# Group norm of the next image inside the attention, and earlier maxima, in a conv, attention and experts kernel

## The chip, the cores and the metric

The kernel runs on one core of a Trainium2 chip. The metric is the time of one execution on the device, in microseconds. The core has TensorE (PE: matmuls, its weight loads listed as PEld), VectorE (DVE), ScalarE (ACT), GpSimd (POOL) and SyncE (SP), which issues DMAs. The engines run their own instruction streams and meet through semaphores. PSUM, where matmuls put their results, has eight banks of 128 x 512 float32.

## The reference, cut to what matters

For each of 8 images x (192 channels, 32 x 32 = 1024 tokens):

```python
x = x + spiking_attention(group_norm(x))   # 32 groups of 6 channels
t = tokens(x)                              # 1024 x 192
t = t + softmax_attention(layer_norm(t))   # 6 heads of 32, causal
t = t + experts(layer_norm(t))             # 4 experts, 192 -> 768 -> 192, the best 2 by a gate

spike(x) = round(clip(x, 0, 4)) / 4
xs = spike(group_norm(x)); q, k, v = spike(conv_bn(xs)); kv = k^T v (by head, 8 heads)
a = spike(q @ kv * scale); out = conv_bn(a)
gate = softmax(x @ gate_w + gate_b), masked to its two largest, normed to a sum of 1
y = sum_e gate[e] * (gelu(x @ w1[e] + b1[e]) @ w2[e] + b2[e])
```

## The kernel before

An image has two stages. In the **attention** (`attend`) 36 steps j go over (block b of 512 queries, pair of heads, chunk kc of 128 keys). In step j PE makes the scores of item j (L474, L478; banks 4 and 5 or 6 and 7, two steps in turn) and, two items behind, the weighted sums of item j-2 (`weigh`, L676; banks 0 and 1, in turn by run, a run being one block and pair). ScalarE makes the exponential of an item (L875), in five buffers. VectorE norms a run's output in three parts (L1283; L1288 and L1292; L1301, which signals `o_done`), one part a step, from three steps behind the run's last item. The first sums of run r wait for the output of run r-2.

In the **experts** (`experts`) 48 chunks i go over (block, expert, 128 of 768 hidden columns), with three chunks of lag behind them. PE's order in chunk i: the hidden product of i (`hidden`, L439, five matmuls), asides due by i-0.5, the expert output of i-3 (`expert_out`, L729, twelve matmuls into banks 2 and 3; with an expert's last chunk four biases, L734), asides due by i. Where i-3 begins an expert, asides due by i come before its output. ScalarE: GELU of i (L895), a scaled float16 copy (L903), then asides due by i. VectorE: asides due by i-0.5, then after an expert's sixth output the accumulation (`add_expert`, four instructions, L1335), then the low half h_l (L1351), then asides due by i. ScalarE thus serves an aside due at a half step at the chunk's end.

Asides are Python generators. `yield T` means that what follows is due at step T; `Aside.until(step)` emits all that is due by then. So the due times in `FRONT_AT` and `TAIL_AT` put each engine's order down in writing, and each engine waits on semaphores besides. `tail` is the output projection, second layer norm, transposes and gate of a block: block 0's runs in the attention (bank 2 and 3, from 18.5), block 1's in the experts (banks 4 and 5, from 4). `front` of the **next** image runs in the experts of this one:

- group norm: statistics of x by channel (L1052 to L1056), two small products with a group matrix (L494, L498, bank 7) that sum over groups, mean and variance (L1059 to L1072), the power -1/2 on GpSimd (L954), a refining step (L1029 to L1077), Relu with scale and bias on ScalarE (L794), rounding on VectorE (L1084, L1086) into xs;
- query (L510), key and value (L523) products of the spikes, their Relus (L801, L809) and roundings; kvm (L534), its split, the attention products (L547), their rounding (L1117, L1120), the projection (L559), the residual t1 (L1129), the first layer norm: statistics (L1010 to L1024), power on GpSimd (L976), normed blocks u (L1039, L1042), transposes (L446) with copies ah (ScalarE, L815) and al (VectorE, L1152); six query-key products (L439) whose high and low halves are written by ScalarE (L821) and VectorE (L1161); value products (L439) and their copy (L830);
- the heads and keys are spread by 24 + 24 DMAs from SyncE and GpSimd;
- the 36 maxima: products of queries and keys (L617, with a mask L621; banks 4 and 5 or 6 and 7 in turn) whose row maxima VectorE takes (L1169). `maximum_step` places them. Of block 0 they are transposed into rows (L454, L782).

The first image's front runs in the setup by the same table, with the pieces of the weights in between. The GpSimd order in an image is: power of norm 1, keys, power of the tail's two blocks, group power of the next image. SyncE's is: spread, then channels and tokens of the next image.

Of the kernel before, what the change touches and what calls it, by code (L numbers as in the profile page):

```python
# [1 line left out]

# [59 lines left out]
           for half in range(b + 1) for pair in range(PAIRS)]  # L62
# [29 lines left out]

PV_BANK = (0, 1, 0, 1, 0, 1)
# [3 lines left out]
def maximum_step(i):  # L97

    return FRONT_AT["maxima"] + int(2 * i / PER_CHUNK) / 2

# [34 lines left out]
def build(nc, x_ch, x_tok, consts, w_conv, bn, w_in, w_out, b1, b2, gate_b, out):  # L135
    with ExitStack() as ctx:
# [218 lines left out]
        y_used = sem("y_used", NB * EXPERTS)  # L355
# [18 lines left out]
        def _(sp):  # L374
            def load(img):
                sp.wait_ge(xs_ready, at(xs_ready, img, 0))
                sp.dma_start(xc[:, :, :], x_ch[img]).then_inc(x_ch_in, 16)
                sp.wait_ge(t1_ready, at(t1_ready, img, 0))
                sp.dma_start(xt[:, :, :], x_tok[img]).then_inc(x_tok_in, 16)
# [50 lines left out]
        def _(pe):  # L430
# [55 lines left out]

            def front(img, later):


                yield FRONT_AT["sums"]  # L490
                pe.wait_ge(gn_rhs, at(gn_rhs, img, 1))
                if later:
                    pe.wait_ge(e_done, at(e_done, img, 0))
                pe.matmul(ps[0:CC, 7, 0:2], group, gn_s[:, :], start=True, stop=True)\  # L494
                  .then_inc(gn_ps, 1)
                yield FRONT_AT["sums2"]
                pe.wait_ge(gn_rhs, at(gn_rhs, img, 2))
                pe.matmul(ps[0:CC, 7, 2:4], group, gn_v[:, :], start=True, stop=True)\  # L498
                  .then_inc(gn_ps, 1)


                for b in range(NB):
                    yield FRONT_AT["q"] + 2 * b
                    if b == 0:
                        pe.wait_ge(xs_ready, at(xs_ready, img, 2))
                    elif later:
                        pe.wait_ge(gate_used, at(gate_used, img, 0))
                    for m in range(2):
                        for n, (w, c) in enumerate(((wc_h, 0), (wc_l, 0), (wc_h, 1), (wc_l, 1))):
                            mm = pe.matmul(ps[0:CC, 6 - 2 * b + m, :], w[0:CC, c, m * CC:(m + 1) * CC],  # L510
                                           xs[0:CC, c, b * QB:(b + 1) * QB], start=(n == 0), stop=(n == 3))
                        mm.then_inc(q_ps, 1)
                for t in range(NT):
                    if t % 2 == 0:
                        yield FRONT_AT["kv"] + t // 2

                    if t < 4:
# [3 lines left out]
                    for n, (w, c) in enumerate(((wc_h, 0), (wc_l, 0), (wc_h, 1), (wc_l, 1))):  # L521
                        rows = CC + 1 if c == 0 else CC
                        mm = pe.matmul(ps[:, 4 + (t + 2) % 4, 0:2 * C], xs[0:rows, c, t * P:(t + 1) * P],  # L523
# [3 lines left out]
                yield FRONT_AT["kvm"] + 0.5  # L527
# [4 lines left out]
                for m in range(2):  # L532
                    for t in range(NT):
                        mm = pe.matmul(ps[0:CC, 4, m * CC:(m + 1) * CC], kvi[:, t, m * CC:(m + 1) * CC],  # L534
# [4 lines left out]
                for b in range(NB):  # L539
                    yield FRONT_AT["attn"] + b  # L540
# [3 lines left out]
                    pe.wait_ge(q_int, at(q_int, img, b + 1))  # L544
                    for m in range(2):
# [5 lines left out]
                for t in range(NT):  # L551
                    if t % TB == 0:
                        yield FRONT_AT["p"] + t // TB
# [12 lines left out]
                for b in range(NB):  # L566
                    yield FRONT_AT["turn"] + b + 0.5
# [4 lines left out]
                for i in range(QK_PARTS * NB):  # L572
                    b, j = divmod(i, QK_PARTS)
                    yield FRONT_AT["qk"] + i // 2 + (0.5 if i % 2 else 0)
# [8 lines left out]
                for t in range(NT):  # L583
                    if t % 4 == 0:
                        yield FRONT_AT["v"] + t // 4
# [8 lines left out]
                for i, (b, t, half, pair) in enumerate(M_ITEMS):  # L594
                    yield maximum_step(i)
# [36 lines left out]
            def tail(img, b, later):  # L632
# [859 lines left out]
```

## Time and profile before

| what | us |
|---|---|
| median of three runs | 1693.17 (1693.16 to 1693.79) |
| the profiled execution | 1693.13 |
| its span | 1691.2 |
| busy in the span: PE, DVE, ACT | 1594.4, 1186.7, 904.3 |
| one image of the steady middle | 201.3 |

Busy time is the union of an engine's instructions. PE's matmuls are pipelined and their ends modelled, so a group's time on PE is read from start to start. An image's times are shown for the one whose experts begin at 771.6 us; its attention begins at 929.4 us and ends at 973.

### The profile page before, as it was taken

Reading aid. Unit: us, or ns where it says so; the run is one execution under the profiler, and the core shown is the slowest. Engines: PE = TensorE matmul, PEld = TensorE weight load, DVE = VectorE, ACT = ScalarE, POOL = GpSimd, SP = SyncE. Lnnn points to the kernel's source line nnn. Section 1 sums busy time; section 2 is a strip of 40 time slices with the busy share of each in tenths; the row PEclk is TensorE's granted clock in tenths of the full one; section 3 lists DMA queues with packets and bytes.
Section 4 is the critical chain, followed back from the end, with each engine's and each line's share of the span. In section 5 each row is a group of like instructions: output and inputs, shape, how many; then the busy total and the mean of one; then the engine's idle time right before and its main releaser. Section 6 shows DMA issues by size and latency. Waiting matters only on the chain.

```text
span 1691.2 us, 32852 instructions
## 1 busy us (share of the span) xinstructions
PE 1594.4 (94%) x13274; PEld 1032.3 (61%) x13274; DVE 1186.7 (70%) x2537; ACT 904.3 (53%) x1329; POOL 173.4 (10%) x247
## 2 busy tenths in 40 slices
PE   3989999999999999999998999999999999999998
PEld 1534666556765576556775566655666557655666
DVE  6677776767676775868758678676767677586643
ACT  3216654466544655356553665446654566535654
POOL 2300111001300003001020010200120000300100
PEclk9999999999999999999999999999999999999999
DMA  4202001100201002010020100210010100200000
GB/s 159 70 13 64 2 16 52 48 2 2 54 14 48 1 1 66 1 48 1 1 67 1 49 2 3 65 33 17 2 46 21 48 2 1 67 1 11 1 11 10
DMA packets 25130, 47.29 MB, mean 28 GB/s; under 512 B 7410, under 2 KB 16946, under 8 KB 23700
## 3 DMA queue, kind: packets, MB, share of 16 engines
q1 hardware_dynamic: 15728, 27.85, 6.0%
q0 software_dynamic: 6144, 9.45, 2.4%
q10 hardware_dynamic: 3108, 7.91, 1.3%
q8 instruction: 104, 1.70, 0.4%
q14 instruction: 46, 0.38, 0.1%
HBM read 19.82 MB, written 6.29 MB: 15 GB/s over the span
## 4 chain that ended last, share of the span: by engine, by line
PE 67%; DVE 23%; ACT 4%; issue 3%; POOL 1%; DMA 1%; SPq 0%; DVEq 0%; ACTq 0%; POOLq 0%
PE ps L439 20%; PE ps L729 16%; PE ps L676 10%; DVE mx L1169 7%; PE ps L474 6%; DVE acc L1335 3%; PE ps L617 3%; DVE room L1351 3%; PE ps L523 2%; DVE norm_stats L1010 2%; PE ps L510 1%; PE ps L446 1%; ACT room L895 1%; PE ps L478 1%; DVE gn_st L1052 1%
## 5 line engine op out<-in xcount | busy, mean ns | idle before, releaser
L895 ACT ACTIVATE room<-ps,b_sb 128x512 f32<-128x512 f32 x384 | 263.3, 686 | 459.4 <-PE ps L439 459.3
L729 PE MATMUL ps<-wout_h,room 128*128 128x192 f16 x3072 | 459.5, 246 | 5.4 <-DVE acc L1335 5.4
L1351 DVE SCALAR_TENSOR_TENSOR room<-room 128x512 f16<-128x512 f32 x384 | 262.6, 687 | 179.3 <-ACT room L903 174.3
L729 PE MATMUL ps<-wout_l,room 128*128 128x192 f16 x1536 | 378.0, 246 | 0.0
L729 PEld LDWEIGHTS ps<-wout_h,room 128*128 128x128 f16 x3072 | 286.5, 98 | 45.8 <-DVE acc L1335 11.8
L875 ACT ACTIVATE room<-ps 128x1024 f32<-128x1024 f32 (+3 forms) x288 | 225.0, 811 | 157.5 <-PE ps L478 120.1
L1169 DVE TENSOR_REDUCE mx<-ps 128x2 f32<-128x1024 f32 (+3 forms) x288 | 264.2, 950 | 33.7 <-PE ps L621 18.1
L903 ACT ACTIVATE room<-room 128x512 f16<-128x512 f32 x384 | 241.9, 630 | 34.0 <-ACT room L895 0.4
L676 PE MATMUL ps<-room,v 128*64 128x512 f32 (+3 forms) x1152 | 232.6, 488 | 0.9 <-DVE o L1301 0.9
L617 PE MATMUL ps<-qk 96*128 96x512 f16 (+3 forms) x576 | 149.0, 328 | 33.2 <-DVE mx L1169 29.0
L729 PEld LDWEIGHTS ps<-wout_l,room 128*128 128x128 f16 x1536 | 150.4, 98 | 27.4 <-issue 0.3
L474 PE MATMUL ps<-qk 98*64 98x512 f16 (+3 forms) x1152 | 156.1, 331 | 10.8 <-DVE mx L1169 8.0
L439 PE MATMUL ps<-uh,win_h 128*128 128x512 f16 x384 | 146.0, 380 | 2.9 <-DVE o L1301 2.9
L439 PE MATMUL ps<-uh,win_l 128*128 128x512 f16 x384 | 145.6, 379 | 0.0
L439 PE MATMUL ps<-ul,win_t 128*128 128x512 f16 x384 | 145.5, 379 | 0.0
L439 PE MATMUL ps<-uh,win_t 128*128 128x512 f16 x384 | 145.5, 379 | 0.0
L439 PE MATMUL ps<-ul,win_h 128*128 128x512 f16 x384 | 145.5, 379 | 0.0
L1335 DVE SCALAR_TENSOR_TENSOR acc<-ps,gate,acc 128x192 f32<-128x192 f32 x256 | 88.9, 409 | 72.4 <-PE ps L734 71.7
L474 PEld LDWEIGHTS ps<-qk 98*64 98x64 f16 x1152 | 61.9, 110 | 93.2 <-issue 47.1
L982 POOL TENSOR_TENSOR norm_pow<-norm_var,minus_half 128x4 f32<-128x4 f32 x16 | 18.6, 1166 | 911.7 <-DVE norm_var L1024 911.7
L617 PEld LDWEIGHTS ps<-qk 96*128 96x128 f16 x576 | 52.2, 98 | 92.4 <-DVE mx L1169 51.7
L676 PEld LDWEIGHTS ps<-room,v 128*64 128x64 f32 x1152 | 66.4, 137 | 29.9 <-issue 3.0
(203 smaller groups left out, 2314.2 us busy)
## 6 DMA issues: line engine op xcount, KB each, us to landing
xc<-x_ch SPq DMA_DIRECT2D x8, 768.0 KB, 5.9
qk<-qk_all SPq DMA_DIRECT2D x96, 64.0 KB, 2.3
qk<-qk_all POOLq DMA_DIRECT2D x96, 64.0 KB, 2.5
out<-acc ACTq DMA_DIRECT2D x16, 384.0 KB, 2.5
xt<-x_tok SPq DMA_DIRECT2D x7, 768.0 KB, 7.1
qk<-qk_all POOLq DMA_DIRECT2D x96, 32.0 KB, 2.0
qk<-qk_all SPq DMA_DIRECT2D x96, 32.0 KB, 2.4
room<-w_in SPq DMA_DIRECT2D x2, 1024.0 KB, 8.7
```

Source lines behind the costliest of these rows:

```text
L439: mm = pe.matmul(dst, lhs, rhs, start=(n == 0), stop=(n == 4))
L474: mm = pe.matmul(ps[keys, bank, q0:QB], k4[:, h, kc * P + keys.start:kc * P + keys.stop], q4[:, h, b * QB + q0:(b + 1) * QB], start=True, ...
L523: mm = pe.matmul(ps[:, 4 + (t + 2) % 4, 0:2 * C], xs[0:rows, c, t * P:(t + 1) * P], w[0:rows, c, C:3 * C], start=(n == 0), stop=(n == 3))
L617: mm = pe.matmul(ps[:, bank, 0:width], q4[0:3 * D, h, t * P:(t + 1) * P], k4[0:3 * D, h, half * QB:half * QB + width], start=True, stop=no ...
L676: mm = pe.matmul(ps[a * 2 * D:(a + 1) * 2 * D, bank, q0:QB], v32[:, kc * PAIRS + pair, a * D:(a + 2) * D], p32[j % N_P32][:, a, q0:QB], st ...
L729: mm = pe.matmul(dst, hid[:, s, tok], w[:, n, :], start=(k == 0 and m == 0 and t % 2 == 0), stop=False, skip_group_check=True)
L875: act.activation(p32[j % N_P32][:, :, q0:QB], ps[:, bank:bank + 2, q0:QB], ACT.Exp, scale=scale).then_inc(e_done, 1)
L895: act.activation(h32[:, i % N_H, :], ps[:, H_BANK[i], :], ACT.Gelu, scale=1 / (U_SCALE * W_SCALE), bias=b1_sb[:, n:n + 1])\
L903: act.activation(h_h[:, i % N_H, :], h32[:, i % N_H, :], ACT.Copy, scale=A_SCALE)\
L1169: V.tensor_reduce(mx[:, half, t, 2 * pair:2 * pair + 2], ps[:, bank:bank + 2, 0:width], AX.X, ALU.max)\
L1335: ins = V.scalar_tensor_tensor(out=acc[:, n, :], in0=ps[:, 2 + t // 2, (t % 2) * C:(t % 2 + 1) * C], scalar=gate[:, n, e:e + 1], in1=acc[: ...
L1351: V.scalar_tensor_tensor(out=h_l[:, s, :], in0=h32[:, s, :], scalar=A_SCALE, in1=h_h[:, s, :], op0=ALU.mult, op1=ALU.subtract)\
```

## The change

- The front's first part, from the statistics to the spikes xs, is taken out as a generator `early`. For images after the first it runs beside `tail` in the attention of the image before (`EARLY_AT`), with the group sums in bank 2 for bank 7. The projection of the tail's block 0, which uses bank 2 too, waits for the group variance.
- What is left of the front gets its own table: queries 4.5 steps sooner, keys and values 3.5, kvm 3, attention to query-key products 1.5, values 2.5, maxima 5. The maxima are set at 2.1 a chunk (2.75 before). Query, key and value products use banks 6 and 7 alone, each waiting for the Relu two products back; kvm goes to bank 6.
- An expert's output signals after its first two token tiles (`y_half`) and at its end; the accumulation runs in two halves, each behind its signal, and PE's next expert waits for them one by one, bank by bank.
- GpSimd's group power stands before the tail's. SyncE loads the channels of the image after the next once the spikes of the next are made, behind its tokens.
- The first image keeps its table under the name `FIRST_AT`, with 2.1 in place of 2.75, whose order there is the same.

```diff
+FIRST_AT = {... as FRONT_AT was, with "relu": 7.5 and "q1": 12.5 ...}
+EARLY_AT = {"stats": 1, "sums": 6, "sums2": 8, "variance": 8, "clip": 10.5, "relu": 11.5, "xs": 13}
+FRONT_AT = {"q": 6, "q1": 8, "q_int": 7, "kv": 9, "kv_int": 9.5, "kvm": 13.5, "kvm_split": 14.5,
+            "attn": 17, "attn_int": 17, "p": 18, "residual": 18, "norm": 20.5, "turn": 22.5,
+            "high": 23.5, "low": 23.5, "qk": 24.5, "qk_lo": 24.5, "v": 27.5, "maxima": 29.5}
-FRONT_AT = {"stats": 3, "sums": 4.5, "sums2": 5.5, "variance": 5.5, "clip": 6, "xs": 8.5,
-            "q": 10.5, "q_int": 11.5, "kv": 12.5, "kv_int": 13, "kvm": 16.5, "kvm_split": 17.5,
-            "attn": 18.5, "attn_int": 18.5, "p": 19.5, "residual": 19.5, "norm": 22, "turn": 24,
-            "high": 25, "low": 25, "qk": 26, "qk_lo": 26, "v": 30, "maxima": 34.5}
-PER_CHUNK = 2.75
+PER_CHUNK = 2.1
+KVM_BANK = 6
+def group_bank(img):
+    return 2 if img else 7
+def query_bank(later, b, m):
+    return 6 + m if later else 6 - 2 * b + m
+def key_value_bank(later, t):
+    return 6 + t % 2 if later else 4 + (t + 2) % 4
...
             load_later(0)
+            load_channels(1)
             for img in range(B - 1):
                 spread(img)
                 if img == 0:
                     load_later(1)
-                load(img + 1)
+                load_tokens(img + 1)
+                if img + 2 < B:
+                    load_channels(img + 2)
...
+            def early(img, when):                      # PE
+                yield when["sums"]
+                pe.wait_ge(gn_rhs, at(gn_rhs, img, 1))
+                if img > 1:
+                    pe.wait_ge(y_used, at(y_used, img - 1, 0))
+                pe.matmul(ps[0:CC, group_bank(img), 0:2], group, gn_s[:, :], start=True, stop=True)\
+                  .then_inc(gn_ps, 1)
+                yield when["sums2"]
...
                     if b == 0:
                         pe.wait_ge(xs_ready, at(xs_ready, img, 2))
+                        if later:
+                            pe.wait_ge(e_done, at(e_done, img, 0))
                     elif later:
-                        pe.wait_ge(gate_used, at(gate_used, img, 0))
+                        pe.wait_ge(q_relu, at(q_relu, img, 2))
...
+                    if later:
+                        pe.wait_ge(*((q_relu, at(q_relu, img, t + 3)) if t < 2 else
+                                     (kv_relu, at(kv_relu, img, t - 1))))
...
                     pe.wait_ge(q_int, at(q_int, img, b + 1))
+                    if b == 0 and later:
+                        pe.wait_ge(gate_used, at(gate_used, img, 0))
...
                 if b:                                  # tail, PE
                     pe.wait_ge(e_done, at(e_done, img, NE))
+                elif img + 1 < B:
+                    pe.wait_ge(var_ready, at(var_ready, img + 1, 1))
...
+                following = Aside(early(img + 1, EARLY_AT) if img + 1 < B else iter(()))
                 for j in range(NE + PV_LAG):
...
                         weigh(j - PV_LAG)
+                    following.until(j)
                     aside.until(j)
...
-                            pe.wait_ge(y_used, at(y_used, img, i // HC))
+                            pe.wait_ge(y_used, at(y_used, img, 2 * (i // HC) - 1))
                     pe.wait_ge(h_lo, at(h_lo, img, i + 1))
                     s = i % N_H
                     for t in range(TB):
+                        if k == 0 and i and t == TB // 2:
+                            pe.wait_ge(y_used, at(y_used, img, 2 * (i // HC)))
...
+                            if t == TB // 2 - 1:
+                                mm.then_inc(y_half, 1)
...
+            def early(img, when):                      # ACT
+                yield when["relu"]
+                act.wait_ge(gn_ready, at(gn_ready, img, 1))
+                if img:
+                    act.wait_ge(a_int, at(a_int, img, 0))
+                for c in range(2):
+                    yield when["relu"] + c
+                    act.activation(tx[:, c, :], xc[:, c, :], ACT.Relu, scale=g_rstd[:, c:c + 1],
+                                   bias=gn_b[:, c:c + 1]).then_inc(x_relu, 1)
...
+                if img + 1 < B:                        # GpSimd
+                    group_power(img + 1)
                 power_of_tail(0)
...
             def add_expert(y):                         # DVE
                 b, e = divmod(y, EXPERTS)
-                dve.wait_ge(f2_done, at(f2_done, img, (y + 1) * HC))
-                for t in range(TB):
+                for half in range(2):
+                    if half == 0:
+                        dve.wait_ge(y_half, at(y_half, img, y + 1))
+                    else:
+                        dve.wait_ge(f2_done, at(f2_done, img, (y + 1) * HC))
+                    if y:
+                        dve.wait_ge(y_used, at(y_used, img, 2 * y - 1 + half))
+                    for t in range(half * TB // 2, (half + 1) * TB // 2):
...
```

VectorE's `early` holds the old lines from the statistics to the two roundings of xs; in its attention loop `following.until(j)` stands behind the norming of a run's output and ahead of the tail's `aside.until(j)`.

## Rows read from the trace of the kernel before

**Rows 1.** Busy us (x instructions) of each engine, clock, DMA: an image, its maxima.

```profile
771.00:972.30 201.30, 194.07 (x1646) 127.00 (x1644) 144.82 (x314) 111.39 (x165) 20.00 (x29) 1.00 0.09 25
...
875.00:929.40 54.40, 49.26 (x416) 33.08 (x414) 44.89 (x65) 21.66 (x32) 0.00 (x0) 1.00 0.00 1
```

**Rows 2.** Who waited for whom, 771.5 to 875: us, times, longest; TensorE's.

```profile
PEld ps L446 <- DVE u L1042: 1.0, 1, 1.0
...
PEld ps L498 <- DVE gn_v L1069: 0.9, 1, 0.9
PEld ps L729 <- DVE acc L1335: 0.9, 1, 0.9
...
PEld ps L439 <- DVE al L1152: 0.5, 1, 0.5
...
PEld ps L439 <- DVE ul L1213: 0.4, 1, 0.4
```

**Rows 3.** The chain that ended last: start, us, what; first and last of the maxima.

```profile
875.58 1.08 PE ps L439 x5
...
877.12 0.99 PE ps L729 x12
...
929.50 0.23 PE ps L474 x2
```

**Rows 4.** Who waited for whom in the maxima, 875 to 929.4.

```profile
PEld ps L617 <- DVE mx L1169: 5.6, 9, 1.8
```

**Rows 5.** Groups by shape in one image: count, busy us, mean ns, idle before.

```profile
L1351 DVE SCALAR_TENSOR_TENSOR room<-room 128x512 f16<-128x512 f32 x48 | 32.8, 686 | 19.1 <-ACT room L903 18.4 <-PE ps L729 0.5
L1169 DVE TENSOR_REDUCE mx<-ps 128x2 f32<-128x1024 f32 x18 | 21.4, 1217 | 1.6 <-PE ps L617 1.4
L1335 DVE SCALAR_TENSOR_TENSOR acc<-ps,gate,acc 128x192 f32<-128x192 f32 x32 | 11.1, 409 | 9.1 <-PE ps L734 9.0
...
L895 ACT ACTIVATE room<-ps,b_sb 128x512 f32<-128x512 f32 x48 | 32.9, 686 | 60.1 <-PE ps L439 60.0
L903 ACT ACTIVATE room<-room 128x512 f16<-128x512 f32 x48 | 30.2, 630 | 4.2
...
L821 ACT ACTIVATE qk_all<-ps 128x512 f16<-128x512 f32 x6 | 3.5, 589 | 2.6 <-PE ps L439 2.6
...
L794 ACT ACTIVATE tmp<-xc,gn_b,g_rstd 96x1024 f32<-96x1024 f32 x2 | 2.5, 1230 | 0.0
```

**Rows 6.** Who waited for whom in the last image's experts, from 1576.

```profile
PEld ps L729 <- DVE acc L1335: 5.5, 6, 1.0
```

**Rows 7.** The chain that ended last, norm of t1 to the transposes.

```profile
835.44 2.10 DVE norm_stats L1010 x8
...
842.83 1.09 PE ps L446 x8
```

**Rows 8.** Timelines at the attention's start: start, us, engine, line [idle before].

```profile
933.88 0.72 DVE L1283 STREAM_TRANSPOSE tmp<-ps 128x512 f32<-128x512 f32 x1 [2.94 <-PE ps L676]
...
936.05 1.39 DVE L1301 TENSOR_TENSOR o<-ps,tmp 32x512 f32<-32x512 f32 x2
...
938.16 1.02 PE L676 MATMUL ps<-room,v 128*64 128x512 f32 x4
...
940.54 2.85 ACT L875 ACTIVATE room<-ps 128x1024 f32<-128x1024 f32 x3 [0.70 <-PE ps L474]
943.57 1.02 ACT L875 ACTIVATE room<-ps 128x1024 f32<-128x1024 f32 x1 [0.18 <-PE ps L474]
...
945.64 0.33 PE L474 MATMUL ps<-qk 98*64 98x384 f16 x2
```

**Rows 9.** Timeline of VectorE, first and last of the group mean's five.

```profile
785.11 0.15 DVE L1059 TENSOR_SCALAR gn_m<-ps 96x2 f32<-96x2 f32 x1
...
785.89 0.16 DVE L1069 TENSOR_REDUCE gn_v<-gn_d 96x2 f32<-96x8 f32 x1
```

**Rows 10.** Groups of ScalarE over the whole span.

```profile
L875 ACT ACT_TABLE_LOAD x8 | 10.3, 1283 | 0.1
```

More of the change, by code:

```diff
@@ L1 @@
 from contextlib import ExitStack
+from itertools import chain
 import numpy as np
@@ L751, in experts @@
                 following.finish()
-            first = Aside(front(0, False))
+            first = Aside(chain(early(0, FIRST_AT), front(0, False)))
             pe.wait_ge(small_in, 16 * n_small)
-            first.until(FRONT_AT["sums"])
+            first.until(FIRST_AT["sums"])
             pe.wait_ge(bn_ready, 2)
@@ L763, in _ @@
             mm.then_inc(bn_ps, 1)
-            first.until(FRONT_AT["sums2"])
+            first.until(FIRST_AT["sums2"])
             pe.wait_ge(consts_ready, 1)
-            first.until(FRONT_AT["turn"])
+            first.until(FIRST_AT["turn"])
             pe.wait_ge(stage_lo, len(pieces))
@@ L919, in _ @@
             act.activation(bn_t[:, 1, :], bn_t[:, 0, :], ACT.Sqrt).then_inc(setup_act, 1)
-            first = Aside(front(0, False))
+            first = Aside(chain(early(0, FIRST_AT), front(0, False)))
             for n, (kind, c0, w) in enumerate(pieces):
@@ L1043, in normalized_block, with spike, early @@
                  .then_inc(signal, 1)
-            def front(img, later):
-                steps = Count()
-                yield FRONT_AT["stats"]
+            tx = tmp[0:CC, 0:2 * N].rearrange("p (c n) -> p c n", c=2)
+            def spike(img, steps, dst, t, signal):
+                V.tensor_scalar(t, t, 4.0, MAGIC, ALU.min, ALU.add).then_inc(front_step, 1)
+                dve.wait_ge(front_step, at(front_step, img, steps.more(1)))
+                V.tensor_scalar(dst, t, MAGIC, None, ALU.subtract).then_inc(signal, 1)
+            def early(img, when, steps):
+                yield when["stats"]
                 dve.wait_ge(x_ch_in, at(x_ch_in, img, 16))
@@ L1145, in front @@
                 for b in range(NB):
-                    yield FRONT_AT["norm"] + b
+                    yield when["norm"] + b
                     normalized_block(norm1, img, t1, b, range(b * TB, (b + 1) * TB), front_step, steps, a_ready)
                 for b in range(NB):
-                    yield FRONT_AT["low"] + b
+                    yield when["low"] + b
                     dve.wait_ge(ah_done, at(ah_done, img, b + 1))
@@ L1272, in tail, with attend @@
                 assert steps.n == (b + 1) * TAIL_STEPS, steps.n
-            def attend(img, later):
+            def attend(img, later, steps):
                 def normalize(run, part):
@@ L1305, in attend @@
                 aside = Aside(tail(img, 0, later))
+                following = Aside(early(img + 1, EARLY_AT, steps) if img + 1 < B else iter(()))
                 ends = run_ends()
@@ L1370, in newton @@
                 step(V.scalar_tensor_tensor(out=into, in0=a, scalar=1.5, in1=y, op0=ALU.add, op1=ALU.mult))
-            first = Aside(front(0, False))
+            steps = Count()
+            first = Aside(chain(early(0, FIRST_AT, steps), front(0, False, steps)))
             dve.wait_ge(rows_in, 16 * n_rows)
             step(V.tensor_scalar(bn_t[:, 0, :], bn_st[:, :, 3], 1e-5, None, ALU.add))
-            first.until(FRONT_AT["stats"])
+            first.until(FIRST_AT["stats"])
             dve.wait_ge(setup_act, 1)
@@ L1384, in _ @@
             step(V.tensor_scalar(q_sb[:, :, 0], bn_t[:, 2, 0:8:4], 1 / SPIKE_SCALE, None, ALU.mult))
-            first.until(FRONT_AT["sums"])
+            first.until(FIRST_AT["sums"])
             dve.wait_ge(small_in, 16 * n_small)
@@ L1388, in _ @@
                 step(V.tensor_scalar(wc[0:CC, c, 0:C], wc[0:CC, c, 0:C], W_SCALE, None, ALU.mult))
-            first.until(FRONT_AT["clip"])
+            first.until(FIRST_AT["clip"])
             dve.wait_ge(bn_ps, 1)
@@ L1400, in _ @@
             V.memset(gate[:, :, :], 0.0).then_inc(consts_ready, 1)
-            first.until(FRONT_AT["xs"] + 1)
+            first.until(FIRST_AT["xs"] + 1)
             step(V.tensor_copy(ident16[:, :], ident))
@@ L1413, in _ @@
                 first.until(PIECE_AT[n])
-            first.until(FRONT_AT["maxima"] - 0.5)
+            first.until(FIRST_AT["maxima"] - 0.5)
             dve.wait_ge(late_in, 16 * n_late)
@@ L1420, in _ @@
             first.finish()
-            attend(0, False)
+            steps = Count()
+            attend(0, False, steps)
             for img in range(B - 1):
-                experts(img, Aside(front(img + 1, True)))
-                attend(img + 1, True)
+                experts(img, Aside(front(img + 1, True, steps)))
+                steps = Count()
+                attend(img + 1, True, steps)
             experts(B - 1, Aside(iter(())))
```

142 lines of the change are left out of this document (68 added, 74 removed).

## The prediction

> **What bounds the kernel now.** I read the busy time of one steady image and of its maxima first, then who waited for whom in each, then the chain that ended last. TensorE (PE) is busy 194.1 of an image's 201.3 us, at the full clock, VectorE 144.8 [rows 1]; the middle images repeat to 0.1 us. So only PE's holes can be won. In the experts' first 104 us there are five short ones, all released by VectorE's chains [rows 2]. Of each such weight-load wait some 0.3 us is the load's head start, so they cost PE about 0.6 (group variance), 0.3 (ul), 0.7 (transposes of u), 0.2 (al) and 0.6 us (an expert's output bank): 2.4 us. The large hole is the maxima: from 875.58 to the scores at 929.50 pass 53.9 us [rows 3]. The work in them is 13 hidden products of 1.08, 16 expert outputs of 0.99 [rows 3] and three biases of 0.33, 36 maxima (12 pairs without a mask at 0.43, six each with one at 0.55, 0.45, 0.34 and 0.24 by width: 14.6 together, an estimate from the spacing of their matmuls), and 1.2 for the row products and two scores: 46.6. **7.2 us are lost**, and the longest wait names VectorE's reductions [rows 4]. The attention has next to no hole on PE: its chain is scores and weighted sums.
>
> **What the change removes.** (a) Group norm and input spikes leave steps 3 to 8.5 of the experts; with them go the wait for the group variance (0.6) and the late ul (0.3): -0.9 us an image. (b) The expert's accumulation frees its two banks one by one. Before, PE had 1.08 us of hidden product to cover 0.2 of hand-over and four accumulations, 0.41 each and 0.33 apart [rows 5]. Now the first bank is free about 0.5 us after PE's last product and the second after 0.95; PE asks at 1.08 and 1.57. Both are in time: -0.6 an image, and in the last image, where nothing fills the boundaries, six waits of 0.9 [rows 6], each 0.6 on PE: -3.6 once. (c) The maxima start five chunks earlier and come at 2.1 a chunk. A wide chunk then asks VectorE for 2 x 1.22 + 0.69 = 3.13 us [rows 5] (back to back each starts 0.08 earlier: 2.9), PE for 2.07 + 2 x 0.49 = 3.05; at 2.75 it was 4.0 against 3.4. Walking items 17 to 35 with these prices leaves 0.3 us for the copied row maxima at item 18, 0.5 at items 21 and 22, which still fall on one half step, and 0.1 at item 33, just behind an accumulation: 0.9 of the 7.2, so **-6.3 an image**. Bounds: 0 and -7.2.
>
> **What it adds between the experts' products.** Attention products, norm and query-key products move 1.5 chunks forward. The distances stay, but where each falls in its chunk changes, and ScalarE serves its asides at a chunk's end alone.
> (d) Norm of t1. Its statistics were due at 21.5, the start of chunk 22; now at 20, the end of chunk 20, behind that chunk's accumulation. From PE's last product of chunk 20 VectorE needs 0.2 + 0.74 (the second bank) + 0.6 (h_l), then the old chain, 7.4 us from the first statistic to the first transposes, GpSimd's power among it [rows 7]: 9.0 with hand-overs. PE reaches the transposes (step 23) after three chunks of 2.07, 6.2. Wait: 2.8, less the old 0.7. Queued on VectorE behind this is h_l of chunk 21, which PE wants three chunks on.
> (e) First query-key product. The copy ah is due at 23.5, which ScalarE serves at the end of chunk 24: from the chunk's start 1.3 (product, hand-over), 0.69 + 0.63 (GELU, its copy), 1.02 for ah (as an exponential of that shape [rows 8]) and 1.22 for al (as a reduction of it), with hand-overs 4.9. PE asks at 1.08 + 0.99 + 0.87 + 1.08 = 4.0. Wait 0.9, less the old 0.2.
> (f) Value products. Now at 27.5, the middle of chunk 28; the second pair needs the bank of query-key item 5. ScalarE's copy of item 5 is due at 24.5 + 3 = 27.5 and so made at the end of chunk 28. From the end of that chunk's hidden product: 0.2 + 0.69 + 0.63 + 0.59 (copy) + 0.69 (VectorE's low half) [rows 5] and hand-overs, 2.9; PE is there after two value tiles, 0.82. Wait **2.1**; before, at step 30, a chunk's end, there was none.
> SyncE's and GpSimd's transfers of heads and keys start 1.5 chunks sooner and the maxima five, so 3.5 chunks of cover go; from query-key item 2 to the first maximum PE still has four chunks and 6.5 us of other products, 14.8 us, for 12 issues and a landing of about 11: hidden, by some 2 us (were it gone, as much an image). GpSimd's group power now stands before the tail's, due ten steps later: nothing. SyncE's load of the next channels waits for the spikes of this image; behind it are only heads of 60 us later: nothing.
> Between the products, old waits taken off: 2.1 + 0.7 + 2.1 = **+4.9** (bounds 0, if VectorE and ScalarE are ahead of where I have them, and +8).
>
> **What it adds in the attention.** The statistics (2.5 us) fit into the 2.94 us that VectorE idles before the first run's transposition [rows 8]. The mean's chain, 0.94 us [rows 9], doesn't: due at step 6, it waits for PE's sum product at 935.3 and ends at 936.3, and the reciprocals that followed the transposition at 934.7 come 1.6 us later. The first output, done at 937.44, is then done at 939.05; the third run wants its bank at 938.16 [rows 8], or 938.4 with the two sum products: +0.7. ScalarE: three exponentials run back to back from 940.54 [rows 8]; two Relus of 1.23 [rows 5] go behind the first and the second, and the scores two steps on need the banks that the late exponentials free. Walking steps 12 to 17: the scores of steps 15 and 16 come at 944.75 and 946.93, and at step 17 PE is at 948.3 instead of 945.64 [rows 8]: 2.7 late, 0.2 of it work moved from the experts, so **+2.5**, the 0.7 among it. From there a wide step of PE (1.3 us) leaves 0.27 over an exponential of 1.03. Bounds: +0.7, if ScalarE's slack takes the Relus, and +5.0, if both land whole.
> The trace shows Relu after GELU without a load and never after an exponential, and eight loads of 1283 ns, one an image, for the exponential's table [rows 10]. The Trainium skill, page "ScalarE: Activation LUTs", section "Table sets: the hidden batching unit", says that cheap functions such as relu are in every set; by it no load is added. No run here shows it for this set, so the other answer stays a rival.
>
> **Sum.** An image: -0.9 - 0.6 - 6.3 + 4.9 + 2.5 = -0.4 us; seven images have it: -2.8. Once: -3.6. From the profiled run's 1693.1 (its span 1691.2 and 1.9 around it; the median of the runs shown, 1693.17, is the same) this gives **1686.7 us**. It is a small difference of terms of 5 us, and each us of error in one is 7 us of time. A measurement of this kernel tells about 0.2%, 3.4 us, from no change.
>
> **Rivals.**
> A, the sum as told, the terms' errors together within 0.8 us an image: 1681 to 1692, chance 0.55, three quarters of it below 1689.8.
> B, the asides run ahead: the waits of (d) to (f) stay at their old size. For it: VectorE is busy 72% of an image, and loses 6 us of work just before. Against: the waits come from ScalarE's service at the chunk's end and from a chain through GpSimd, not from VectorE's load. Without the 4.9: -5.3 x 7 - 3.6, 1652; with half of it, 1670. Chance 0.19, half for each.
> C, slower: ScalarE becomes the bound of the attention's steps 12 to 17. Both Relus land whole on PE (2.46) and so do the two late outputs (1.6 and 0.9): 5.0 for 2.5. It decides once a Relu meets less than 1 us between an exponential's end and the scores that need its bank; the three back-to-back exponentials speak for it, the 0.4 us idle soon after against. +2.1 x 7 - 3.6: 1704. Chance 0.12.
> D, the maxima stay VectorE's: the wide ones still queue behind h_l and accumulation, and half of (c) comes. 2.9 to 3.13 against 3.05 is no margin; the double bank, which lets it lag a reduction, speaks against. +2.8 x 7 - 3.6: 1709. Chance 0.05.
> E, the waits change places alone and (b) is taken up behind them: 1690 to 1696, no difference. Chance 0.07.
> F, two loads around the Relus, 2.6 us an image: +15, 1706. Chance 0.02.
> Faster: three quarters of A and B, 0.6. Same: the rest of A and E, 0.2. Slower: C, D and F, 0.2. The range takes in B's half and C and leaves out B's whole, D and F, 0.16: 1668 to 1705.
>
> **What would show it.** Right: no wait before L617 above 0.5 us; waits on VectorE of 2.8 us before the transposes of u and 2.1 inside the value products; a gap before the weighted sums of the third run and two late scores; no wait of the expert outputs in the last image; an image of 201 us. Wrong: value products without a gap (B), an attention more than 3 us longer (C), L617 waiting over 3 us an image (D), more than 17 table loads (F).

## The result, and the profile after

The changed kernel takes **1704.33 us**, the median of four runs (1703.48 to 1705.87), against 1693.16 us for the kernel before (four runs, 1691.89 to 1693.79): a ratio of 1.0065, 95% interval 1.005 to 1.008. It is slower, where 1686.7 and rather faster was forecast. The profiled execution took 1705.87 us, its span 1703.8, 12.6 more than before. PE's granted clock over the span is 0.991, where it was 0.996.

A steady image of after, and its maxima, which now begin 60.1 us ahead of the attention, as in [rows 1] (stretch in us, length, then busy us and instructions of PE, PEld, DVE, ACT, POOL, then clock and DMA):

```profile
1143.60:1346.36 202.76, 194.13 (x1646) 127.03 (x1644) 145.46 (x314) 111.62 (x165) 20.23 (x29) 1.00 0.09 25
1286.30:1346.40 60.10, 58.22 (x504) 40.45 (x504) 49.91 (x76) 27.33 (x40) 0.04 (x1) 1.00 0.03 8
```

PE's work is that of before, 194.1 us, and this image is 1.5 us longer: its holes grew from 7.2 to 8.6 us. Images of after aren't all alike, though. This one and one other take 202.8 us; the rest of the steady ones take 203.7 to 204.5 and have in them what the forecast knew nothing of, a stretch at half clock.

Who waited for whom between the products of this image, 1189.5 to 1286 us, as in [rows 2] (us in all, times, longest):

```profile
PEld ps L473 <- DVE u L1096: 2.5, 1, 2.5
...
PEld ps L466 <- DVE qk_all L1217: 2.1, 1, 2.1
...
PEld ps L466 <- DVE al L1208: 1.2, 1, 1.2
```

L473 are the transposes of u, L466 with qk_all the value products, L466 with al the first query-key product. The waits for the group variance and for an expert's output bank no longer appear. From 1286 us to the image's end, as in [rows 4]:

```profile
PEld ps L653 <- DVE mx L1225: 3.1, 3, 1.6
```

So L653, the maxima, waits 3.1 us where the same line waited 5.6 us before. In the last image's experts (from 1593.5 us, [rows 6] before) the expert outputs no longer appear; the two longest waits of the weight loads are these:

```profile
PEld ps L466 <- DVE o L1357: 0.9, 1, 0.9
...
PEld ps L466 <- ACT room L948: 0.4, 1, 0.4
```

The chain from the statistics to the transposes, as in [rows 7] (start, us, what):

```profile
1250.31 0.60 DVE room L1414
1250.91 2.10 DVE norm_stats L1064 x8
...
1254.01 1.65 POOL norm_pow L1029
...
1256.28 1.26 DVE u L1093 x4
...
1257.92 1.09 PE ps L473 x8
```

Statistics and transposes are 7.0 us apart, 7.4 before. The attention, as in [rows 8] (four rows of ScalarE, then three of PE):

```profile
1156.45 1.23 ACT L839 ACTIVATE tmp<-xc,gn_b,g_rstd 96x1024 f32<-96x1024 f32 x1
1157.58 1.01 ACT L927 ACTIVATE room<-ps 128x1024 f32<-128x1024 f32 x1
1158.49 1.23 ACT L839 ACTIVATE tmp<-xc,gn_b,g_rstd 96x1024 f32<-96x1024 f32 x1
1159.62 2.87 ACT L927 ACTIVATE room<-ps 128x1024 f32<-128x1024 f32 x3
...
1153.10 1.08 PE L714 MATMUL ps<-room,v 128*64 128x512 f32 x4 [0.43 <-DVE o L1357]
...
1158.64 0.62 PE L501 MATMUL ps<-qk 98*64 98x512 f16 x4 [0.25 <-ACT room L927]
1160.68 0.41 PE L501 MATMUL ps<-qk 98*64 98x512 f16 x2 [0.56 <-ACT room L927]
```

The two Relus (L839) stand among the exponentials, two score products (L501) are late behind them, and the third run's weighted sums (L714) are late behind the first output. And the half clock: stretches of PE alone (length, busy us and instructions, granted clock, DMA), first the end of one image's wait with the transposes behind it, then the 3.4 us after that, then the same place of the undisturbed image:

```profile
1052.90:1055.20 2.30, 1.02 (x9) 1.00 0.00 0
1055.20:1058.60 3.40, 3.40 (x16) 0.50 0.00 0
1258.90:1262.30 3.40, 3.40 (x29) 1.00 0.01 2
```

After a wait of 2.4 us at the full clock, the clock granted is half, 1.2 GHz, for 3.4 us, and 16 matmuls are issued where the undisturbed image issues 29. That image's part up to the first maximum takes 98.06 us instead of 97.09. It happens in five of the seven images with this wait, begins within 1.1 us of the wait's end, and costs 1.0 to 1.7 us each, 6.7 in all.

### The profile page after: what moved, and what is told of

The parts are those of the page before. It is cut to its first block, busy times and chain, and to the rows that moved or that the text cites. A ratio compares the mean times of both kernels' runs of the same rounds, so it can differ in the third digit from the quotient of the medians.

```text
span 1703.8 us, 32914 instructions
## 1 busy us (share of the span) xinstructions
PE 1601.4 (94%) x13274; PEld 1037.6 (61%) x13274; DVE 1192.0 (70%) x2537; ACT 906.3 (53%) x1329; POOL 175.2 (10%) x247
## 4 chain that ended last, share of the span: by engine, by line
PE 78%; DVE 13%; ACT 4%; issue 4%; POOL 1%; DMA 1%; DVEq 0%; ACTq 0%; POOLq 0%
PE ps L466 25%; PE ps L771 20%; PE ps L714 9%; PE ps L501 5%; PE ps L653 5%; DVE mx L1225 3%; PE ps L557 2%; DVE acc L1398 2%; PE ps L473 2%; PE ps L541 1%; ACT room L927 1%; PE ps L681 1%; PE ps L595 1%; PE ps L682 1%; DVE o L1357 1%
## 5 line engine op out<-in xcount | busy, mean ns | idle before, releaser
L1225 DVE TENSOR_REDUCE mx<-ps 128x2 f32<-128x1024 f32 (+3 forms) x288 | 268.4, 954 | 50.6 <-PE ps L657 40.5
L714 PE MATMUL ps<-room,v 128*64 128x512 f32 (+3 forms) x1152 | 232.5, 487 | 5.9 <-DVE o L1357 5.4
L653 PE MATMUL ps<-qk 96*128 96x512 f16 (+3 forms) x576 | 152.6, 329 | 16.7 <-DVE mx L1225 15.3
L501 PE MATMUL ps<-qk 98*64 98x512 f16 (+3 forms) x1152 | 156.2, 331 | 9.3 <-ACT room L927 6.0
L466 PE MATMUL ps<-uh,win_h 128*128 128x512 f16 x384 | 146.9, 383 | 2.9 <-DVE o L1357 2.9
L466 PE MATMUL ps<-uh,win_t 128*128 128x512 f16 x384 | 146.7, 382 | 0.0
L466 PE MATMUL ps<-ul,win_t 128*128 128x512 f16 x384 | 146.7, 382 | 0.0
L466 PE MATMUL ps<-ul,win_h 128*128 128x512 f16 x384 | 146.6, 382 | 0.0
L466 PE MATMUL ps<-uh,win_l 128*128 128x512 f16 x384 | 146.5, 382 | 0.0
L501 PEld LDWEIGHTS ps<-qk 98*64 98x64 f16 x1152 | 61.2, 109 | 92.1 <-issue 41.5
L653 PEld LDWEIGHTS ps<-qk 96*128 96x128 f16 x576 | 54.2, 98 | 68.5 <-DVE mx L1225 32.9
L714 PEld LDWEIGHTS ps<-room,v 128*64 128x64 f32 x1152 | 65.9, 137 | 38.1 <-DVE o L1357 10.8
L505 PE MATMUL ps<-mask_kq,identb 128*64 128x128 bf16 x768 | 78.3, 220 | 0.0
```

The source lines that it names most:

```text
L466: mm = pe.matmul(dst, lhs, rhs, start=(n == 0), stop=(n == 4))
L501: mm = pe.matmul(ps[keys, bank, q0:QB], k4[:, h, kc * P + keys.start:kc * P + keys.stop], q4[:, h, b * QB + q0:(b + 1) * QB], start=True, ...
L505: mm = pe.matmul(ps[keys, bank, q0:q0 + P], identb[:, keys], mask_kq[:, :], start=False, stop=True)
L653: mm = pe.matmul(ps[:, bank, 0:width], q4[0:3 * D, h, t * P:(t + 1) * P], k4[0:3 * D, h, half * QB:half * QB + width], start=True, stop=no ...
L714: mm = pe.matmul(ps[a * 2 * D:(a + 1) * 2 * D, bank, q0:QB], v32[:, kc * PAIRS + pair, a * D:(a + 2) * D], p32[j % N_P32][:, a, q0:QB], st ...
L1225: V.tensor_reduce(mx[:, half, t, 2 * pair:2 * pair + 2], ps[:, bank:bank + 2, 0:width], AX.X, ALU.max)\
```

## The experiments

All are one core and timed in three rounds; ratios are to the kernel before on the same chip. Lengths of an image are read from start of attention to start of attention, of one that has no half clock unless the text says so. "Lost" means PE's time from start to start above what the same matmul takes unhindered.

**The banks by halves alone**, in the kernel before: `y_half`, `y_used` counted twice an expert, and the accumulation in two halves, and nothing else of the change.

> The kernel before with one part of the change alone: an expert's output signals after its first two token tiles, and the accumulation frees its two banks one by one. Group norm, due times and maxima as before. W: six waits of 0.6 us in the last image and one in each image before go, -3.6 - 7 x 0.6 = -8: 1685. Rival: in the images with maxima VectorE is late anyway and the boundary wait only moves into the maxima: -3.6 alone, 1689.6.

1685.92 us, ratio 0.9948 (0.9933 to 0.9963). The image falls from 201.28 to 199.98 us, the last image's experts from 114.7 to 110.5. So this part is a gain of its own, 1.3 us an image where 0.6 was in the sum and 4.2 once where 3.6 was. The whole run could have gained more but for the clock: in four images a wait of 1.65 us in the maxima, which the kernel before has too, is followed by 3.4 us at half clock, 1.7 us lost each; before, that happened in one.

**The group norm in the attention, without the rest**: the kernel after with the old times of the chain and the old rate.

```diff
-            "attn": 17, "attn_int": 17, "p": 18, "residual": 18, "norm": 20.5, "turn": 22.5,
-            "high": 23.5, "low": 23.5, "qk": 24.5, "qk_lo": 24.5, "v": 27.5, "maxima": 29.5}
+            "attn": 18.5, "attn_int": 18.5, "p": 19.5, "residual": 19.5, "norm": 22, "turn": 24,
+            "high": 25, "low": 25, "qk": 26, "qk_lo": 26, "v": 30, "maxima": 34.5}
...
-PER_CHUNK = 2.1
+PER_CHUNK = 2.75
```

> The kernel after, with the chain from the attention products to the maxima at its old due times and the maxima at their old rate of 2.75 from 34.5: so group norm and spikes in the attention and the banks by halves alone are left of the change. The three waits between the experts' products should be as in the kernel before (0.7 and 0.2 us, none in the value products). Theory M (losses in the maxima come from their rate and where they meet the rest of VectorE's work): the maxima lose 7.2 us as before; an image is that with the banks alone, 199.98, less 0.9 for the group norm gone, plus 2.7 in the attention: 201.7 to 201.9, in all about 1697 to 1700. Rival N (taking the group norm out already lets VectorE run ahead in the maxima): losses of 5.3 us, as with the early start at this rate, and images of 199.9, about 1685.

1695.34 us, 1.0004 (0.9993 to 1.0015); the image is 201.80, the middle of theory M, though the whole is 2 us below M's 1697 to 1700. The part up to the first maximum is 0.9 us shorter than with the banks alone, and the attention 2.7 longer. Those two terms add up, and the maxima didn't move:

```profile
PEld ps L653 <- DVE mx L1225: 5.6, 9, 1.8
```

**The rate alone** put back to 2.75 in the kernel after.

> The kernel after, with the maxima 2.75 a chunk as in the kernel before instead of 2.1 (they start at 29.5 as in the kernel after). Theory M (the rate is what made VectorE late): a wide chunk asks VectorE for 4.0 us against 3.4 of TensorE, so the losses inside the maxima come back from 2.5 to about 7.2 us an image; with the half-clock stretches left as they are, 7 x 4.7 = 33 us more than the kernel after: 1735 to 1739. Rival N (the loss of the kernel before came from where the maxima met the other chains, not from the rate; the earlier start and the work taken out of VectorE's way did it): losses of 2.5 to 4 us an image, 1704 to 1715.

1722.32 us, 1.017 (1.0154 to 1.0185). Neither number came: the image is 205.50, 2.7 us longer than after's, where M wanted 4.7 and N at most 1.5. The maxima lose 5.3 us here. Counted alike, they lose 6.6 before, 6.4 in the run just above, 5.3 with the early start at the old rate, and 2.5 with both. So the start five chunks earlier is worth 1.1 us and the rate 2.7: 3.9 together.

**The copy of query-key item 5** half a chunk sooner, ahead of the value products:

```diff
-                    yield when["qk"] + (i + 1) // 2
+                    yield when["qk"] + ((i + 1) // 2 if i < 5 or not later else 2.5)
```

> The changed kernel with one due time moved: ScalarE's copy of query-key item 5 at 27 instead of 27.5, so at the end of chunk 27 and no longer at the end of chunk 28. Theory W (the changed kernel loses its gain in three waits between the experts' products, which each cost what the trace shows): the wait of 2.1 us inside the value products goes in all seven images and nothing takes its place, 1704.3 - 7 x 2.1 = 1689.6, within 2 us; an image shorter by 2.1. Rival R (the slowdown sits in the attention and in VectorE's maxima, and what is taken from a wait before them comes back there): the maxima stage grows by what the value products give, and the time stays above 1700.

1690.52 us, 0.9971 (0.9962 to 0.998). The image is 200.68, 2.08 less than after's, and the wait of L466 for qk_all is gone from the trace. Term (f) is confirmed in place and size.

**The copy ah** at 23 (`"high": 23`), so that ScalarE serves it a chunk sooner.

> The changed kernel with ScalarE's copies ah due at 23 and 24 instead of 23.5 and 24.5, so at the end of the chunk in which the transposes are made. W: the wait of 0.9 us before the first query-key product goes, 1704.3 - 6.3 = 1698, and no more, since the longer waits stand elsewhere. R: no change beyond 1 us, since VectorE's low half then comes at the same time as before or the wait moves on to the value products.

1696.65 us, 1.0014 (1.0004 to 1.0023); image 201.84, 0.92 less. Term (e) too.

**Attention products to norm sooner**: `"attn": 16, "attn_int": 16, "p": 17, "residual": 17, "norm": 20`.

> The changed kernel with attention products, projection and residual one step earlier (16, 17) and norm at 20, so that the statistics of t1 stand ahead of the accumulation of chunk 20 and the norm behind it. W: the wait of 2.4 us before the transposes of u shrinks to 0.3 or less; 7 x 2.2 = 15 us go. With it go the stretches of 3.4 us at half clock that follow this wait in five of the seven images and cost 1.0 to 1.7 us each, 6 to 7 us together: 1704.3 - 22 = 1682. If the half-clock stretches come anyway (rival H: they belong to the load, not to the wait), 1689. R: above 1700.

1695.33 us, 1.0006 (0.9996 to 1.0015), a miss: the image is 202.17, 0.6 less, not 2.4. The transposes don't wait any more, but PE does, for an expert's output bank (waits from 1181.5 to 1278 us):

```profile
PEld ps L771 <- DVE acc L1398: 2.2, 2, 2.0
```

The statistics, 3.1 us of VectorE, now stand ahead of the accumulation of the same chunk, and the wait changed its place. There it costs 1.84 us, 1.7 of them in one standstill, and in none of the seven images does the clock fall. The 9 us against after come from these two: seven times 0.6, and the 6.7 us that after loses to the clock (the spans differ by 10.4).

**The Relus later** in the attention (`"relu": 18, "xs": 25`), and then **sums, variance and clip too** (`"sums": 13, "sums2": 15, "variance": 15, "clip": 17`).

> The kernel after, with the two Relus of the next image's spikes in attention step 18 instead of 11 (and what follows them in step 25 instead of 13); statistics, sums and clip stay. Theory R (the prediction's: steady attention is 2.7 us longer than before, most of it because the Relus delay the exponentials of steps 12 to 17, the rest because of the first output behind the mean's chain, 0.7): with the Relus gone from those steps the attention of an image falls from 45.6 to 44.0 to 44.5 us, and seven images by 8 to 11 us: about 1695. Rival S (the statistics and sums on VectorE and TensorE make the delay, the Relus have slack): the attention stays at 45.3 to 45.6 and the time within 2 us of the kernel after, 1704. Rival T (wherever the Relus stand they cost their 2.5 us of ScalarE): the same 45.6, with the late scores in steps 18 to 24.

> The kernel after, with the sums of the group norm in attention steps 13 and 15, variance 15, clip 17, the Relus in 18 and what follows in 25; the statistics stay in step 1. Theory R: both delays go, that of the first output (0.7 to 1.2 us) and that of the exponentials, and of the attention's 2.7 us only the moved sum products are left: 43.1 to 43.3 us, 0.7 to 1.2 less than with the Relus alone moved; in all 17 us less than the kernel after: about 1687. Rival S (the statistics make the delay): the attention stays above 44.5. Rival T: 45.6 as in the kernel after.

1695.87 us, 1.0014 (1.0005 to 1.0023), and 1689.19 us, 0.9974 (0.9963 to 0.9985). The attention of after, with the late Relus and with all of it late:

```profile
1143.60:1189.19 45.59, 44.06 (x414) 22.40 (x412) 32.34 (x89) 29.90 (x39) 1.73 (x2) 1.00 0.14 45
```

```profile
1137.21:1181.62 44.41, 43.68 (x414) 22.61 (x412) 32.37 (x89) 29.98 (x39) 1.72 (x2) 1.00 0.15 46
```

```profile
1129.65:1173.10 43.45, 43.24 (x416) 22.65 (x412) 32.39 (x89) 29.97 (x39) 1.72 (x2) 1.00 0.16 47
```

Same work, different places: the Relus cost 1.2 us where the change puts them, the sums' chain 1.0, and 0.5 are left over the 42.9 of an attention without any of it. Both S and T fall. In steps 18 and 19 the Relus meet narrow exponentials (0.60 and 0.37 us), and ScalarE idles 1.98 us behind the second of them, so there they cost next to nothing.

**The wait filled.** Ten products nobody reads, inside the wait ahead of the transposes, in the kernel after:

```diff
+                    if later and b == 0:
+                        pe.wait_ge(t1_ready, at(t1_ready, img, 1))
+                        for _ in range(10):
+                            pe.matmul(ps[:, 4, :], win_h[:, 0:P], win_h[:, 0:QB], start=True, stop=True)
                     pe.wait_ge(a_ready, at(a_ready, img, b + 1))
```

> The kernel after, with ten products of 512 columns, whose result nobody uses, issued on TensorE ahead of the transposes of u of images 2 to 8, into the bank that the transposes overwrite; they lie inside the wait of 2.4 us (ten at 216 ns are 2.2 us). Theory H (the half clock comes because TensorE stands still for 2.4 us): the transposes start when they started before, and the half-clock stretches behind them go: all images 202.8 us, 6 to 7 us less in all, about 1697 to 1698. Rival P (the half clock comes from what runs there, the transposes themselves or the chip's load, and not from the standstill): stretches stay in about 5 of 7 images, 1702 to 1705. If the ten products don't fit, up to 0.3 us an image are added under either.

1699.20 us, 1.0028 (1.0018 to 1.0038). The span is 1697.3, 6.5 less than after's, with more work on PE and nothing else touched. One image, all of it (PE, 1656 matmuls for 1646):

```profile
1138.34:1341.10 202.76, 196.29 (x1656) 1.00 0.09 25
```

The image's length is after's to 0.01 us, so the chain behind the wait is what it was; but now all six steady images have this length, and from 150 us on no half clock is granted until the kernel's end. The mean clock of its nine executions is 0.995 to 0.997, that of after's four 0.991. So without PE's standstill those stretches don't come. P falls: the transposes are still there, in the same place. That they have a part in it when they follow a standstill isn't excluded; the stretches of the combined kernel below follow a standstill without them.

**All mends together**: item 5, ah, the norm's sums and Relus late, and the attention products at 15.5 with the statistics at 18.5 and the norm at 19.

> The kernel after with four moves of due times: the copy of query-key item 5 half a chunk sooner and the copy ah at 23 (both as in the first two runs), the norm's statistics for t1 at 18.5 and the norm at 19 with the attention products at 15.5 (one chunk sooner than a chunk's accumulation would ask for, so that neither waits for the other), and the next image's sums, clip and Relus late in the attention, as in the run with all of them late. Theory W (every microsecond lost is a wait between TensorE's products, and the half clock follows the wait before the transposes): from an undisturbed image of 202.8 go 2.1 (item 5), 0.9 (ah), 2.4 (transposes) and 2.5 (attention), 194.9 an image, and the half-clock stretches of the images too: 1648 to 1655. Rival X (the wait before the transposes goes over to the accumulation again, 1.8 us an image as when the norm alone was moved two chunks): 196.7 an image, 1661 to 1666. Rival Y (with the waits gone the maxima lose more, VectorE being the next bound, since less is lost ahead of them): losses in the maxima above 4 us an image, 1665 to 1675.

1684.20 us, 0.9945 (0.9928 to 0.9962). This is rival X, and worse than it said: undisturbed the image is 199.33. The norm at 19 puts the accumulation behind the wait for GpSimd's power (waits from 971 to 1066 us):

```profile
PEld ps L771 <- DVE acc L1398: 3.5, 2, 3.3
...
PEld ps L583 <- DVE kv_l L1168: 1.3, 1, 1.3
```

PE loses 3.0 there and 0.9 before the attention products, and the clock falls after the first in six of seven images.

**Statistics and norm parted**: attention products at 16 again, the statistics at 18.5 (`yield when["residual"] + 1.5`), the norm at 20, so that VectorE makes the accumulation while GpSimd makes the power. **Then the rate** at 2.0.

> As the combined run before, but the attention products at 16 again and the norm's statistics at 18.5 with the norm itself at 20, behind the chunk's accumulation, so that the accumulation doesn't stand behind the wait for GpSimd's power. Theory W: the wait of 3.0 before an expert's output and that of 0.9 before the attention products go, and with the first the half clock of six images: 199.33 - 3.0 - 0.9 = 195.4 us an image, 1645 to 1650. Rival X (one of the two takes a new place: transposes wait, or the accumulation still does): 1 to 2 us an image more, 1655 to 1662, with half-clock stretches where the wait is above 1.6 us.

> The run before this one with the maxima at exactly two a chunk, so that no half chunk takes two of them. Theory M (the losses at items 20 to 22 come from the half step with two maxima, that at item 33 from its place behind an accumulation): 0.5 us an image less for the doubled step, and of the 1.25 at item 33 all if it comes off the accumulation: 193.6 to 195 an image, 3 to 12 us less than the run before it. Rival N (TensorE waits for the accumulation's chunk however the maxima stand): no difference, within 2 us of that run.

1646.02 us, 0.9715 (0.9698 to 0.9731), and 1639.19 us, **0.9675** (0.9658 to 0.9692), the fastest. A steady image of each:

```profile
904.53:1099.83 195.30, 192.84 (x1646) 127.34 (x1644) 145.65 (x314) 111.75 (x165) 20.64 (x29) 1.00 0.10 26
```

```profile
900.24:1094.53 194.29, 192.48 (x1646) 127.58 (x1644) 145.76 (x314) 111.86 (x165) 20.63 (x29) 1.00 0.09 26
```

PE's holes are down to 2.5 and 1.8 us an image, all images have the full clock, and between an attention's end and the first maximum nothing of the front makes PE wait. W's forecast of 195.4 was met to 0.1 us. The rate of 2.0 takes another 1.0 us off the image, more than the doubled half step's 0.5 and less than that with all of item 33's 1.25: 0.7 is now lost at item 31 and 0.7 at the first score behind the maxima. The 6.8 us lie inside M's 3 to 12.

## Why the prediction was wrong, step by step

The steps, an image, with what was measured:

| step | forecast | measured | read from |
|---|---|---|---|
| (a) group norm out of the experts | -0.9 | -0.9 | norm alone against banks alone |
| (b) banks by halves | -0.6, once -3.6 | -1.3, once -4.2 | banks alone |
| (c) maxima | -6.3 | -3.9 (by the images' lengths -3.7) | losses, norm alone to after |
| (d) transposes of u | 2.8 - 0.7 | 2.4 - 0.7 | trace of after |
| (e) first query-key product | 0.9 - 0.2 | 0.9, the 0.2 went with (b) | trace, ah early |
| (f) value products | 2.1 | 2.05 | trace, item 5 |
| attention | +2.5 | +2.7 | Relus and sums late |
| sum | -0.4 | +1.3 (the image: +1.5) | |
| half clock, in all | none | 6.7, before 1.7 | filled wait |

**The step that failed is (c).** The maxima were said to lose 7.2 us and to keep 0.9. They lost 6.6, because 0.6 of the 7.2 were short waits among scores that after has as well; 0.2 of it went with (b); and they keep 2.5. The largest of these is item 33, sized at 0.1 "just behind an accumulation". The rows around it (start, us, engine; the last is PE's weight load for it):

```profile
1331.19 1.38 DVE L1398 SCALAR_TENSOR_TENSOR acc<-ps,gate,acc 128x192 f32<-128x192 f32 x4
...
1332.49 0.68 DVE L1414 SCALAR_TENSOR_TENSOR room<-room 128x512 f16<-128x512 f32 x1
...
1333.09 2.35 DVE L1225 TENSOR_REDUCE mx<-ps 128x2 f32<-128x1024 f32 x2
...
1334.36 0.10 PEld L653 LDWEIGHTS ps<-qk 96*128 96x128 f16 x1 [1.57 <-DVE mx L1225]
```

Four accumulations and an h_l stand ahead of the two reductions; item 33 needs the bank that the first of them frees and comes 1.25 us late. That the accumulation makes the wait is read from the order of these rows; no run moved it alone. The walk compared a chunk's work, 3.13 us of VectorE against 3.05 of PE. That is for two maxima a chunk; with the prediction's own prices 2.1 make 3.25 against 3.10, and neither counts the accumulation, 1.38 us every sixth chunk, or 0.23 a chunk. By this estimate VectorE has no slack among the wide maxima; from 1320 to 1336 us the trace has it busy 14.6 of 16 us, PE 14.9. Item 8 (0.5) wasn't in the walk. In all (c) falls 2.4 us an image short, 17 in seven, of the 19.2 between 1686.7 and the profiled 1705.9.

**The second is the clock**, a term that the sum didn't have. The trace of before showed it, once: the one image with a half-clock stretch, at 310 us, behind a wait of 1.65 us, against six without (another lies at 118.8 us, where the first attention begins). A change that puts a wait of 2.4 us into every image pays for more than the wait. This is 6.7 us for 1.7, 5 more.

**Against these stood (b)**, undersized by 0.7 an image and 0.6 once, 5.5 us: the wait for the bank showed 0.6 on PE, but with it went 0.3 at ul, 0.15 at al and 0.2 at item 12 of the maxima. That these queued behind the accumulation on VectorE is argued, not shown; what is shown is that they are gone with the banks alone. (a) had counted ul as its own and is right in size because the two sum products, 0.2, left with the norm. With these, 17 + 5 - 5.5 = 16.5 of the 19.2 are told. The set-up before the first attention is 2.2 us longer (half-clock stretches lie elsewhere); the experiments' own first attentions begin from 120.1 to 122.7 us, so what of it the change makes stays open.

**What held.** The three waits came at the places named and within 0.4 us of their size, with the reasons named: moving the two copies took two of them away exactly. The attention's 2.7 is right in sum, and its parts differ a little: 1.0 for the sums' chain (0.7 forecast), 1.2 for the Relus (1.8), and 0.5 for the rest, the moved products' 0.2 in it. Nor is any transfer of heads or keys waited for.

Of the marks for being right two failed: the longest wait before L653 is 1.6 us where 0.5 was allowed, and the image is 202.8, not 201.

**The rivals.** A, the sum as told, falls with (c) and the clock. B falls: the value products have their gap. C named the measured time, 1704, by coincidence: the attention grew by 2.7, not 5. E falls, its waits weren't only moved. D, that half of (c) is lost, is what came nearest (3.9 of 6.3 gained, where D had 3.1), with the accumulation and h_l as it said, and had a chance of 0.05; its mark, L617 waiting over 3 us an image, is met at 3.1, barely. F falls: the exponential's line loads its table as often as in [rows 10], and the loads are 17 in all. (Its price was also added up wrong: 2.6 us in seven images on top of 1686.7 is 1705, not 1706.)

```profile
L927 ACT ACT_TABLE_LOAD x8 | 10.3, 1283 | 0.1
```

That agrees with the Trainium skill, page "ScalarE: Activation LUTs", section "Table sets: the hidden batching unit", that relu is in every set: two Relus between exponentials brought no load.

The chances were wrong in kind, too: seven terms of which the two largest, -6.3 and +4.9, nearly cancel, each good to 1 or 2 us, leave a sum of -0.4 without a sign. The range (1668 to 1705) said so; 0.6 for faster did not.

## What to carry to other kernels

When two engines share a chunk's time, add up all their work at the rate that is set, the rare lumps too (here an accumulation of 1.4 us), and walk the queue in its order. Put work that waits for a third engine in two pieces with the lump between them: this and the attention products half a chunk later took the combined kernel from 199.33 to 195.30 us an image. Changes that come together should be tried apart: the banks alone gained some 8 us, and due times that were off by half a chunk to some chunks cost the changed kernel 65 (1704 to 1639, the rate of 2.0 among it). Where PE had to wait, filling the wait with products nobody reads cost nothing in the image's length and took 6.5 us of half clock off the span.

## What the runs showed of the hardware

The granted clock of TensorE can fall to half after quite short waits in a kernel in which it is busy 94% of the time, and does so in some images and not in others, though the images are alike to 0.01 us. Each such stretch lasted 3.4 us and cost 1.0 to 1.7 us. Counted over all runs, images in which a half-clock stretch follows the wait named:

| PE's loss in the wait | kernels | images with a stretch |
|---|---|---|
| 3.0, before an expert's output | combined | 6 of 7 |
| 2.4, before the transposes | after, ah early, item 5, Relus late, all late, rate 2.75 | 5, 3, 2, 4, 3, 4 of 7 each |
| 1.7, before an expert's output | norm sooner | 0 of 7 |
| 1.65, in the maxima | before, banks alone, norm alone | 1, 4, 1 of 7 each |
| under 1.3 | the two last | 0 of 14 |
| 2.4, of it 2.2 filled (other waits up to 2.05) | filled wait | 0 of 7 |

The waits of 2.05 us in the value products, in every image of after and of all the runs with them, were never followed by a stretch. Outside this count, the first image's attention has a wait of 2.57 us for a run's output in the eight kernels with the sums at steps 6 and 8, and a stretch follows it in four of them (item 5, norm sooner, rate 2.75, filled wait), in after not. Why a wait of 1.65 in the maxima is followed by a stretch and the 2.05 and the 1.7 before an expert's output aren't was not tried; nor is it shown what decides between two equal images.
